# Softmax sums of two 16-head attention loops inverted in a 64-row layout, with a transfer there and one back

## The reference, cut to what matters

```python
q = split(q @ Wq.T + bq)              # 16 heads of 8, 56 queries a batch
k = split(ctx @ Wk.T + bk)            # 1500 keys
v = split(ctx @ Wv.T + bv)
scores = q @ k.T / sqrt(8)            # masked in L1
attn = softmax(scores, axis=-1)
out = (attn @ v) @ Wo.T + bo
```

## Time and profile before

| | |
|---|---|
| median of 3 runs | 3889.08 us |
| lowest and highest | 3884.86 and 3899.47 us |
| the profiled execution's own time | 3887.87 us |
| its span, first to last instruction | 3886.1 us |
| busy: TensorE, VectorE, ScalarE, GpSimd | 3344.9, 2514.8, 2066.9, 1154.1 us |
| the L1 loop's sums, first and last reciprocal | 471.0 and 1236.2 us |

### The profile page before, as it was taken

How to read it: one execution, slowest core, us unless ns; L and a number is a source line. 1 busy time by engine, 2 the same in 40 slices (tenths; PEclk the granted TensorE clock), 3 DMA queues, 4 the chain that set the end, 5 groups by cost and what they waited for, 6 DMA issues and landing times. The chain is left out here.

```text
span 3886.1 us, 96641 instructions
## 1 busy us (share of the span) xinstructions
PE 3344.9 (86%) x40650; PEld 2451.9 (63%) x40650; DVE 2514.8 (65%) x3568; ACT 2066.9 (53%) x3842; POOL 1154.1 (30%) x1125
## 2 busy tenths in 40 slices
PE   6776799999998575999999996579999999999988
PEld 4455577777776563777777774346666666666654
DVE  5633577677774224777777773667878878778751
ACT  3211366566664111666566663367677776776733
POOL 0012312222121214222222111135455455554520
PEclk9877899999999686999999997689999999999989
DMA  7932666555561314555554530100000000000000
GB/s 226 254 120 72 176 165 167 157 150 157 162 167 31 106 38 116 129 132 133 124 124 123 129 92 7 22 24 17 25 25 17 24 18 23 25 17 25 17 1 26
DMA packets 137255, 345.88 MB, mean 89 GB/s; under 512 B 56179, under 2 KB 79547, under 8 KB 136827
## 3 DMA queue, kind: packets, MB, share of 16 engines
q1 hardware_dynamic: 134139, 334.22, 32.3%
q0 software_dynamic: 2688, 5.51, 0.5%
HBM read 174.63 MB, written 17.09 MB: 49 GB/s over the span
## 5 line engine op out<-in xcount | busy, mean ns | idle before, releaser
L2040 POOL TENSOR_TENSOR l_S<-l_S,l_shift 125x448 f32<-125x448 f32 (+1 forms) x416 | 461.1, 1147 | 329.0 <-ACT l_shift L2272 326.5
L1338 ACT ACTIVATE L1a_probs<-ps 125x448 f32<-125x448 f32 x768 | 383.2, 544 | 202.8 <-PE ps L1238 189.5
L1338 ACT ACTIVATE L2a_probs<-ps 125x448 f32<-125x448 f32 x768 | 382.9, 544 | 203.3 <-PE ps L1238 189.9
L1371 DVE TENSOR_REDUCE L2a_chunk_max<-ps 112x1 f32<-112x1000 f32 x256 | 300.9, 1196 | 147.4 <-PE ps L1197 147.0
L1371 DVE TENSOR_REDUCE L1a_chunk_max<-ps 112x1 f32<-112x1000 f32 x256 | 300.9, 1196 | 135.9 <-PE ps L1197 135.4
L2150 PE MATMUL ps<-l_S,l_z 125*128 125x448 f32 x768 | 344.3, 545 | 0.0
L2253 ACT ACTIVATE ctx_stats<-ps 125x512 f32<-125x512 f32 (+1 forms) x416 | 248.3, 597 | 180.0 <-PE ps L2098 170.8
L2317 DVE TENSOR_REDUCE l_norms<-ctx_stats 125x8 f32<-125x512 f32 (+1 forms) x416 | 268.1, 675 | 77.9 <-ACT ctx_stats L2253 77.8
L2343 DVE SCALAR_TENSOR_TENSOR l_S<-ps,l_neg_cols,l_inv_norms 125x448 f32<-125x448 f32 x384 | 256.1, 679 | 81.8 <-PE ps L2119 77.1
L1197 PE MATMUL ps<-L1a_keys,L1a_queries 98*112 98x500 f32 x768 | 264.6, 427 | 47.0 <-DVE L1a_chunk_max L1371 20.5
L1197 PE MATMUL ps<-L2a_keys,L2a_queries 96*112 96x500 f32 x768 | 264.6, 427 | 45.8 <-DVE L2a_chunk_max L1371 20.5
(11 more groups left out here) (478 smaller groups left out, 7071.3 us busy)
## 6 DMA issues: line engine op xcount, KB each, us to landing
L1a_keys<-L1a_k_hi SPq DMA_DIRECT2D x256, 187.5 KB
L2a_keys<-L2a_k_hi SPq DMA_DIRECT2D x256, 187.5 KB
a_ctx_T<-in_ctx_T SPq DMA_DIRECT2D x32, 750.0 KB, 11.7
L1a_ctx_T<-in_ctx_T SPq DMA_DIRECT2D x32, 750.0 KB, 6.1
xn<-L_valid SPq DMA_DIRECT2D x32, 750.0 KB, 7.6
L1a_keys<-L1a_k_lo SPq DMA_DIRECT2D x128, 187.5 KB
L2a_ctx_T<-in_ctx_T SPq DMA_DIRECT2D x32, 750.0 KB, 6.4
L2a_keys<-L2a_k_lo SPq DMA_DIRECT2D x128, 187.5 KB
```

Source lines behind the costliest of these rows:

```text
L1338: nc.scalar.activation(probs[t % NPR][:, h * HQ // 2:(h + 1) * HQ // 2], s.ps[0:KP, i % 3, 0:HQ // 2], ACT.Exp).then_inc(probs_made, 1)
L1371: ins = nc.vector.tensor_reduce(chunk_max[:, n, 0:1], product, AX.XY, ALU.max)
L2040: nc.gpsimd.tensor_tensor(S[b % 2][0:r, t, :], S[b % 2][0:r, t, :], shift[0:r, :], ALU.add)\
```

## The change

The item "sums" moves from step 5 to step 9, after row item 11. For every batch but the last of each loop it is made another way: SP moves the 4 rows of sums out of `acc` into a tile `sums` of 64 rows of 14; VectorE inverts that into `inv_sums` after the row item of step 6 (`INVERT_AT`); SP moves the result back into the 4 sum rows of `inv`, whose other rows are zeroed once by a new memset; TensorE spreads `inv` with the same product as before; and VectorE multiplies `acc` by that product, straight from PSUM. Both of SP's transfers are issued in `turn_sums`, which stands behind the loads of b+3 and ahead of the maxima transfers. The last batch goes the old way.

```diff
-    step_items[5].append(("sums", -1, 0))
+    step_items[9].append(("sums", -1, 0))
+    INVERT_AT = 6
...
+        sums, inv_sums = sb("sums", [64, SQ // 4]), sb("inv_sums", [64, SQ // 4])
...
+            def turn_sums(b):
+                sp.wait_ge(acc_taken, b + 1)
+                if b:
+                    sp.wait_ge(inverted, b)
+                sp.dma_start(sums[:, :], acc[DK:D:32, :]).then_inc(sums_moved, 16)
+                sp.wait_ge(inverted, b + 1)
+                if b:
+                    sp.wait_ge(products, made[("sums", b - 1, 0)])
+                else:
+                    sp.wait_ge(prep, 4)
+                sp.dma_start(inv[DK:D:32, :], inv_sums[:, :]).then_inc(inverses_moved, 16)
...
                     load_terms(b + 3)
+                if b:
+                    turn_sums(b - 1)
                 if b + 1 < B:
                     move_maxima(b + 1)
...
-                if b == 0:
-                    pe.wait_ge(prep, 3)
-                pe.wait_ge(acc_taken, b + 1)
+                if b == B - 1:
+                    pe.wait_ge(acc_taken, B)
+                    by_row = acc
+                else:
+                    pe.wait_ge(inverses_moved, 16 * b + 16)
+                    by_row = inv
                 nc.tensor.matmul(s.ps[:, bank(item), 0:4 * SQ], sum_rows[:, :, :].rearrange("p j i -> p (j i)"),
-                                 acc[:, :], start=True, stop=True).then_inc(products, 1)
+                                 by_row[:, :], start=True, stop=True).then_inc(products, 1)
...
-                    act.wait_ge(normed, b)
+                    act.wait_ge(scratch_dve, by_dve[("sums", b - 1, 0)])
...
+                if b < B - 1:
+                    nc.vector.tensor_tensor(here, whole, s.ps[:, bank(item), 0:4 * SQ].rearrange("p (c q) -> p c q", c=4),
+                                            ALU.mult).then_inc(scratch_dve, 1)
+                    return
+                dve.wait_ge(products, made[("sums", b - 1, 0)])
                 nc.vector.reciprocal(inv[:, :], s.ps[:, bank(item), 0:4 * SQ]).then_inc(scratch_dve, 1)
...
+            def invert_sums(b):
+                dve.wait_ge(sums_moved, 16 * b + 16)
+                if b:
+                    dve.wait_ge(inverses_moved, 16 * b)
+                nc.vector.reciprocal(inv_sums[:, :], sums[:, :]).then_inc(inverted, 1)
...
+            nc.vector.memset(inv[:, :], 0.0).then_inc(prep, 1)
...
                 for t in range(KT):
                     for item in of_batch(b, step_items[t]):
                         empty(item)
+                    if t == INVERT_AT and b:
+                        invert_sums(b - 1)
```

More of the change, by code:

```diff
@@ L991, in attention_16_heads @@
             sem(n) for n in ("k_hi_made", "k_lo_made", "queries_made", "max_made", "hi_split", "row_moved", "scores_made"))
-        probs_made, probs_used, acc_taken, normed = (
-            sem(n) for n in ("probs_made", "probs_used", "acc_taken", "normed"))
+        probs_made, probs_used, acc_taken, normed, sums_moved, inverted, inverses_moved = (
+            sem(n) for n in ("probs_made", "probs_used", "acc_taken", "normed", "sums_moved", "inverted", "inverses_moved"))
         weights_loaded, mask_loaded, quads_loaded, zeroed, cut, prep, q_product, q_made, q_split = (
@@ L1157, in _ @@
             pool.wait_ge(ones_set, NQ + 4)
-            pool.wait_ge(prep, 3)
+            pool.wait_ge(prep, 4)
             for b in range(B):
@@ L1398, in norm @@
                     dve.wait_ge(terms_stored, 96)
+                here, whole = heads_out[:, :, b * SQ:(b + 1) * SQ], acc[:, :].rearrange("p (c q) -> p c q", c=4)
+                if b < B - 1:
[3 more added lines that the diff above has]
+                dve.wait_ge(products, made[("sums", b - 1, 0)])
                 nc.vector.reciprocal(inv[:, :], s.ps[:, bank(item), 0:4 * SQ]).then_inc(scratch_dve, 1)
                 dve.wait_ge(scratch_dve, by_dve[item])
-                nc.vector.tensor_tensor(heads_out[:, :, b * SQ:(b + 1) * SQ], acc[:, :].rearrange("p (c q) -> p c q", c=4),
-                                        inv[:, :].rearrange("p (c q) -> p c q", c=4), ALU.mult).then_inc(normed, 1)
+                nc.vector.tensor_tensor(here, whole, inv[:, :].rearrange("p (c q) -> p c q", c=4), ALU.mult)\
+                    .then_inc(normed, 1)
+            def invert_sums(b):
[3 more added lines that the diff above has]
+                nc.vector.reciprocal(inv_sums[:, :], sums[:, :]).then_inc(inverted, 1)
             def empty(item):
```

## The result

The changed kernel takes 4056.9 us (median of 4 runs, 4047.3 to 4063.0) against 3888.3 us: a ratio of 1.0426, 95% interval 1.0394 to 1.0459, so 4.3% slower. The forecast was 4100 us in a range of 3970 to 4190. The profiled execution took 4047.3 us, 159.4 more than that of before.

The account below looks back on a forecast made before the run. TensorE's one instruction stream was taken to bound the kernel. Waiting of 168 us, 45 for the clock and -2 for other batches gave +211 on 3889, so 4100 us, range 3970 to 4190.

Parts of the forecast that it names:

- The bound and what is removed: Both loops: TensorE's stream bounds; dropping 62 long reciprocals returns 81 us to VectorE, and only the item's placing counts.
- on-time gain: Per batch, if both new transfers are on time: keys product earlier by about 0.4 us, bounds 0 and 0.79.
- Where SP stands: SP's queue: sums go out behind keys, context, validity and q_terms, whose last issue ends at mean R+0.8 (L1), R-0.2 (L2).
- R: Start of the old 128x224 reciprocal in a batch; R+x is x us after it.
- The landing: Sums' transfer out, behind q_terms in the loaded queue: lands at R+6.2 in L1 and R+4.4 in L2.
- Rival C: No queueing: sums land 2.05 us after their issue; L1 loses 0.9, L2 gains 0.1 a batch, 3911 us; chance 0.08.
- What waits for it: VectorE waits before row items 9 to 11, delaying TensorE's keys product: +3.9 us a batch in L1, +2.1 in L2.
- T: Time at which the sums' outgoing transfer lands; keys product put at T + 3.75, break-even at T = R+2.3.
- The clock: TensorE's stalls of 4.1 (L1) and 2.3 us (L2) drop its clock: 1.0 and 0.6 us a batch, bounds 0 and 1.6.
- The sum: 28 batches a loop: 168 us waiting, 45 clock, -2 for six other batches; +211 on 3889, so 4100 us.
- Rival A: Transfers wait but the clock holds: 4055 us; chance 0.24.
- Rival D: Sums land before R+2.3 in both loops, VectorE never waits: -25 us, or -49 at the bound, 3840 to 3864; chance 0.06.

Follow-up runs that it names:

- the place alone: Kernel before the change with only the item sums moved from step 5 to step 9, old reciprocal, no transfers: 3884.6 us, ratio 0.9984.
- nobody waiting: Changed kernel with both transfers into spare tiles, inverted tile and spread factor constant, so no wait for a landing: 3882.9 us, ratio 0.9986.
- both transfers early: Changed kernel with sums out ahead of the keys, inversion after step 3, transfer back between keys and loads: 3870.6 us, ratio 0.9958.
- the filler run: Changed kernel with ten 128x128 products without a reader ahead of row product 11 in L1's loop alone: 4038.1 us, ratio 1.0377.

## Why the prediction was right, point by point

**The bound and what is removed** held: TensorE's one stream sets the time, and 92 us less of VectorE bought nothing by themselves. The on-time gain of 0.4 us a batch measured 0.35 in most batches (24.95 against 25.3 with the place alone, with nobody waiting, and with both transfers early). In the mean over all batches it was less: between none and 0.11 with the place alone and with nobody waiting, 0.25 and 0.34 with both early. In the last two batches measured of each loop, without keys, the changed kernel gained 0.7 to 0.9.

**Where SP stands** held: the sums' issue begins at R+1.4 in the batch shown, R+1.2 had been counted.

**The landing** was the right mechanism with too large a size. It was put at R+6.2 and R+4.4; the inversions begin at 19.84 and 17.99 us after the maxima (medians), so R+5.2 and R+3.3, about 1 us earlier in both loops. The step that was off is "from the last q_terms' landing plus 0.3 us". The last q_terms landed about when they had been put, 20.7 and 18.7 us after the maxima (R+6.0 and R+4.0, for R+5.9 and R+4.1). But the sums didn't stand behind them to the end: in 24 of 28 L1 batches and 25 of 28 L2 batches VectorE inverted before the last q_terms had landed, by a median 0.7 and 0.8 us. In the batch shown the three q_terms took from issue to landing
```profile
DMA to landing us min/median/max: 4.6/6.1/6.2
```
so the last one, issued at 859.99, landed at 866.2, and the inversion started at 864.38, 3.8 us after the start of the sums' own issue. The load ahead made the sums late, then, but not by a strict order of landings. The Trainium skill (DMA: Bandwidth & Descriptors, "Why a DMA increments its semaphore by 16 and not by 1") says that a transfer issued by SP uses the largest number of DMA engines, up to 16, that divides the slowest dimension on both sides, which would be 4 for 4 rows and 64 rows against 16 for the q_terms. That would let the sums land once 4 engines are through their share of the load, which is an inference. The run with 16 rows has that number at 4 too, so no run here separates this from other causes, and it stays open. Rival C, the constant of some 2 us, is by a fit of the Trainium skill (DMA: Bandwidth & Descriptors, "Anatomy of one DMA"), which that page gives for transfers issued by GpSimd and not by SP; for a loaded queue of SP the 3.8 us here and the run with the sums between keys and loads refute it.

**What waits for it** held step by step: VectorE in order, the bank of row item 9, TensorE at row product 11, and the keys product 3.64 us after the inversion's start where the clock stays up (3.90 in the median L1 batch) for T + 3.75. The way back was put at T + 2.9 and took 2.2 where it was the last to come (854.68 to 856.85 in the run with the inversion after step 8). TensorE's stall was put at 4.1 and 2.3 us and is 3.0 and 0.9 in the mean of those it had (72.8 us in 24 waits, 20.5 in 22, each in a stretch of 700 us). Per batch up to the keys product: forecast +3.9 and +2.1, measured +3.0 and +0.8. T's miss of 1.0 and 1.1 us is nearly all of that.

**The clock** was put at 1.0 and 0.6 us a batch and measured about 1.25 and 0.37; in sum 1.6 both times. That the sums agree is luck: L1 was put too low and L2 too high. The slow stretch could be longer than in the earlier trace rows: in the batch shown it lasts from 865.2 to 872.0. The Trainium skill (TensorE: Matmul & The Clock Gate, "Part 1: The HAM clock gate") calls half clock the state of an idle TensorE; the filler run's clock, 0.97 in place of 0.91 in L1 with less idle time, agrees.

**The sum**: 28 x (3.9 + 2.1 + 1.6) - 2 = 211, measured 159 in the profiled execution and 169 between the medians. Rival A's 4055 us is next to the measured 4057, but not for its reason: the clock did fall. T, put about 1 us too late, is what left the forecast 43 us too high. Rival D, the faster side, needed a landing before R+2.3; the changed kernel had them at R+5.2 and R+3.3, and only with SP's order changed did the sums come in time, at 3871 us, and at 3847 with the item in step 7.

## What to carry to other kernels

Here a small transfer cost what stood just ahead of it in its queue, or nearly: look up, for the very place of its issue, how long the neighbours take to land, before hanging an in-order engine on it. Here the same two transfers were worth +169 us behind the loads and -19 ahead of them, and -46 with the item at a place where other work follows. In this kernel a wait on an engine with time to spare reached the bounding engine through the buffers that it empties, and the slower clock behind the stall was a part of the price; and the short item was worth 65 us in step 7, where its length mattered, and 14 in step 9, where it didn't.

## What the runs showed of the hardware that had not been expected

A tiny transfer back to SBUF with an empty queue landed 1.3 us after its issue ended (855.54 to 856.85), faster than the 2.05 of the earlier trace rows. Moving 3.5 KB in 64 pieces or in 16 made no difference to the landing (120.2 and 121.3 us of waits in 29). The sums' transfer, issued behind the q_terms, landed before the last of them in 49 of 56 batches. Ten added matmuls a batch left the program no slower, with the granted clock at 0.97 instead of 0.91.
